# Sigmoid centres by tanh on GpSimd, the second attention's row norms on GpSimd and its row statistics a step later, and capacity blocks normed one at a time

## What is computed

```python
x = layernorm(x + L0_attn(x)); x = layernorm(x + L0_ffn(x))
x = layernorm(x + L1_attn(x)); x = layernorm(x + L1_ffn(x))
# L1_attn, what matters here (16 heads of width 8):
c = tanh(mixed_q @ wfq + bfq + (glo @ wfg + bfg))
P = sigmoid(sum(c * up)) * key_len      # centre of each row's window
Z = sigmoid(sum(c * uz)) * key_len      # its width
scores = q @ k.T / sqrt(8) - (j - P)**2 * 2 / Z**2
ctx = softmax(scores) @ v; return ctx @ wo + bo
# L1_ffn: each row goes to its best expert of 8, 160 slots an expert;
# rows that find no slot keep a zero contribution
```

## Time and profile before

| | before |
|---|---|
| median of 3 runs | 1567.42 us (1565.87 to 1569.64) |
| the profiled execution's own time | 1567.29 us |
| its span | 1565.5 us |
| PE busy | 1419.6 us, 91% |
| DVE busy | 1107.7 us, 71% |
| ACT busy | 996.5 us, 64% |
| POOL busy | 876.5 us, 56% |
| mean granted clock of PE | 0.959 of full |

### The profile page before, as it was taken

One profiled execution on the slowest core, in us unless ns is written; L12 is line 12 of the kernel. 1 busy time (PEld: TensorE's weight loads), 2 busy tenths in 40 slices (PEclk: granted clock), 3 DMA queues, 4 the chain that ended last, 5 costly groups with the idle time before them and its releaser, 6 DMA issues. The chain is left out here.

```text
span 1565.5 us, 37854 instructions
## 1 busy us (share of the span) xinstructions
PE 1419.6 (91%) x12163; PEld 805.0 (51%) x12163; DVE 1107.7 (71%) x2545; ACT 996.5 (64%) x2144; POOL 876.5 (56%) x1078
## 2 busy tenths in 40 slices
PE   5999999999999999999978999888889889897825
PEld 3666666666666666666646776623333333332215
DVE  5657676676766667676677898878887887888623
ACT  2666665666566566656647888747777777775612
POOL 4676777677677767767775445622342342342643
PEclk8999999999999999999989999969999999999967
DMA  6100000010000011000100000131111111112100
GB/s 194 32 22 22 24 26 20 20 27 20 20 21 26 20 20 27 20 20 20 27 14 5 0 0 1 41 87 49 45 34 52 36 35 50 30 43 73 29 14 27
DMA packets 74396, 50.83 MB, mean 32 GB/s; under 512 B 31099, under 2 KB 63728, under 8 KB 74192
## 3 DMA queue, kind: packets, MB, share of 16 engines
q1 hardware_dynamic: 71232, 45.70, 10.7%
q10 hardware_dynamic: 1760, 3.02, 0.6%
q0 software_dynamic: 1344, 1.33, 0.3%
HBM read 38.18 MB, written 13.28 MB: 33 GB/s over the span
## 5 line engine op out<-in xcount | busy, mean ns | idle before, releaser
L2031 DVE TENSOR_REDUCE a_nm<-a_s 128x1 f16<-128x512 f32 x512 | 323.7, 685 | 61.7 <-PE a_s L1853 59.0
L620 ACT ACTIVATE prob<-score_ps,nmax 128x512 f32<-128x512 f32 (+3 forms) x512 | 266.8, 528 | 149.5 <-DVE nmax L692 149.5
L692 DVE TENSOR_REDUCE nmax<-score_ps 128x1 f32<-128x512 f32 (+3 forms) x512 | 224.9, 480 | 184.5 <-PE score_ps L498 179.6
L1989 ACT ACTIVATE a_pt<-a_st 128x1024 f32<-128x1024 f32 x256 | 261.5, 1023 | 107.9 <-PE a_st L1857 106.4
L1853 PE MATMUL a_s<-a_kop,a_qop 64*128 64x512 f16 x512 | 185.9, 408 | 48.4 <-DVE a_nm L2031 40.9
L510 PE MATMUL pt_ps<-ident,prob 128*128 128x128 f32 x1280 | 182.7, 273 | 2.6 <-ACT pt L629 1.4
L629 ACT ACTIVATE pt<-pt_ps 128x512 f32<-128x512 f32 (+1 forms) x192 | 102.9, 536 | 123.7 <-PE pt_ps L510 123.7
L1889 PE MATMUL a_pv<-a_pt,a_vaug 128*32 128x256 f32 x2048 | 170.6, 406 | 8.9 <-ACT a_pvs L1994 7.6
L817 POOL TENSOR_SCALAR_AFFINE_SELECT k_h<-k 64x512 f16<-64x512 f32 x130 | 80.8, 622 | 170.7 <-ACT k L653 158.2
L1857 PE MATMUL a_st<-a_qop,a_kop 64*128 64x512 f16 x512 | 175.3, 399 | 0.0
L510 PEld LDWEIGHTS pt_ps<-ident,prob 128*128 128x128 f32 x1280 | 145.6, 141 | 35.2 <-ACT pt L629 1.6
(11 more groups left out here) (390 smaller groups left out, 3252.8 us busy)
## 6 DMA issues: line engine op xcount, KB each, us to landing
r_bc<-r_parts SPq DMA_DIRECT2D x128, 128.0 KB, 2.8
a_qop<-q_parts SPq DMA_DIRECT2D x64, 64.0 KB, 1.9
a_kop<-k_parts SPq DMA_DIRECT2D x64, 64.0 KB, 1.9
e_w<-in_L_ffn_w_dram SPq DMA_DIRECT2D x16, 256.0 KB, 3.3
x_tok<-in_L_attn_input_dram SPq DMA_DIRECT2D x4, 512.0 KB, 13.1
r_parts<-rsum SPq DMA_DIRECT2D x128, 2.0 KB, 2.1
q_parts<-a_q_h SPq DMA_DIRECT2D x16, 128.0 KB, 2.3
k_parts<-a_k_h SPq DMA_DIRECT2D x16, 128.0 KB, 2.3
```

Source lines behind the costliest of these rows:

```text
L620: ins = nc.scalar.activation(prob[h][:, P_OFF[c]:P_OFF[c] + w], score_ps[u][:, col:col + w], ACT.Exp, bias=nmax[h][:, c:c + 1], accum_out= ...
L692: ins = nc.vector.tensor_reduce(nmax[h][:, c:c + 1], score_ps[u][:, col:col + P * (c + 1)], AX.X, ALU.max, negate=True)
L1989: nc.scalar.activation(pt[kc % 2][r][:, :, :], st_ps[r][:, :, :], ACT.Exp, scale=1.0 / SC).then_inc(exp_done[r], 1)
L2031: nc.vector.tensor_reduce(nm[g % 2][:, c, hh:hh + 1], s_ps[j][:, :], AX.X, ALU.max, negate=True).then_inc(max_done[j], 1)
```

## The change

The centre is computed from a tanh: sigmoid(x) is 1/2 + tanh(x/2)/2. ACT now runs a Tanh on the centre's half and an Exp on the width's half of the same product. DVE's three operations for them are gone; POOL does a gate, the +1 on the width's half and one multiply-add that makes `a_cent`, ahead of its coefficients. DVE takes the row statistics of `OUT` in slot 11 in place of slot 10. The norm `a_xn` is made by POOL, behind `a_rstd` and ahead of the `a_scale` operations. In the capacity stage each block has its own `c_var`, `c_rstd`, `c_res` and scatter; POOL raises the next block's variance before it scatters the one before.

```diff
         def sigmoids(kind, b, nb):
             act.wait_ge(coef_done, nb)
             used(kind, b, "PZ")
-            nc.scalar.activation(epz[:, :, :].rearrange("p c h -> p (c h)"), misc[:, 0:QC * 2 * H1], ACT.Exp,
-                                 scale=-1.0).then_inc(misc_out, 1)
+            pz = misc[:, 0:QC * 2 * H1].rearrange("p (c h) -> p c h", c=QC)
+            nc.scalar.activation(epz[:, :, 0:H1], pz[:, :, 0:H1], ACT.Tanh, scale=0.5)
+            nc.scalar.activation(epz[:, :, H1:], pz[:, :, H1:], ACT.Exp, scale=-1.0).then_inc(misc_out, 1)
...
-        def centres(kind, b, nb):
-
-            steps = Steps(dve, cf_steps, 2 * nb)
-            dve.wait_ge(coef_done, nb)
-            dve.wait_ge(misc_out, use(kind, b, "PZ") + 1)
-            steps.step(nc.vector.tensor_scalar(epz[:, :, :], epz[:, :, :], 1.0, None, ALU.add))
-            steps.step(nc.vector.reciprocal(cent[:, :, :], epz[:, :, 0:H1]))
-            nc.vector.tensor_scalar(cent[:, :, :], cent[:, :, :], S / 32.0, -(S - 1) / 64, ALU.mult, ALU.add).then_inc(cent_done, 1)
...
             if j == 0:
-                pool.wait_ge(cent_done, nb + 1)
+                pool.wait_ge(misc_out, use(kind, b, "PZ") + 1)
+                pool_gate(nc, m, slice(0, P))
+                centre = Steps(pool, cf_steps, 2 * nb)
+                centre.done(nc.gpsimd.tensor_scalar(z, z, 1.0, None, ALU.add))
+                centre.step(nc.gpsimd.tensor_scalar(c, epz[:, :, 0:H1], S / 64.0, 1.0 / 64, ALU.mult, ALU.add))
...
+
+            def statistics(kind, b):
                 dve.wait_ge(misc_out, use(kind, b, "OUT") + 1)
-                layer_norm_stats(nc, dve, m, 2 * B + cb, y, st, mv)
-
-            def norm(cb):
-                layer_norm_apply(nc, dve, m, 2 * B + cb, y, mv, rstd, xn).then_inc(ln_dve, 1)
+                layer_norm_stats(nc, dve, m, 2 * B + b - 1, y, st, mv)
...
             def slot(kind, b, at):
                 if kind == "first" and at == 9:
                     last_stats()
+                if kind != "first" and at == 11:
+                    statistics(kind, b)
...
             def output(kind, b, cb):
                 layer_norm_gpsimd(nc, pool, m, 2 * B + cb, mv, ve, rstd)
                 pool.wait_ge(m.rstd_ready, 2 * B + cb + 1)
+                pool_gate(nc, m, slice(0, P))
+                for c in range(QC):
+                    last = nc.gpsimd.tensor_scalar(xn[:, c, :], y[:, c, :], mv[:, c, 0:1], rstd[:, c:c + 1], ALU.subtract, ALU.mult)
+                last.then_inc(ln_dve, 1)
...
                 steps.step(nc.vector.bn_aggr(mv[:, c, :], st[:, c, :]))
-
-            def variance(i):
-                two = slice(*PAIRS1[i])
-                nc.vector.tensor_tensor(var[:, two], mv[:, two, 1], m.eps[:, 0:PAIRS1[i][1] - PAIRS1[i][0]], ALU.add).then_inc(var_ready, 1)
...
+                nc.vector.tensor_tensor(var[:, c:c + 1], mv[:, c, 1:2], m.eps[:, 0:1], ALU.add).then_inc(var_ready, 1)
...
             for q in range(4):
                 tokens(q)
-            for i, blocks in enumerate(PAIRS1):
-                for c in range(*blocks):
-                    finish(c)
-                variance(i)
-                if i < len(PAIRS1) - 2:
-                    normalise(i)
-            for i in range(len(PAIRS1) - 2, len(PAIRS1)):
-                normalise(i)
+            finish(0)
+            for c in range(1, CH):
+                finish(c)
+                normalise(c - 1)
+            normalise(CH - 1)
...
             pool.wait_ge(tokens_done, 4)
-            for i in range(len(PAIRS1) - 2):
-                inverse_deviation(i)
-                scatter(i)
-            for i in range(len(PAIRS1) - 2, len(PAIRS1)):
-                inverse_deviation(i)
-            for i in range(len(PAIRS1) - 2, len(PAIRS1)):
-                scatter(i)
+            inverse_deviation(0)
+            for c in range(1, CH):
+                inverse_deviation(c)
+                scatter(c - 1)
+            scatter(CH - 1)
```

More of the change, by code:

```diff
@@ L1265, in ahead @@
                 if i in PARTS_AT:
[L1266 removed]
+                    turns["PZ_part"](PARTS_AT[i], "prep0", 0, 0)
                 if i == 0:
@@ L1375, in gauss_memory @@
                          "pool_steps"))
-    g.cf_steps, g.coef_done, g.vaug_done, g.ln_dve, g.pv_mm, g.parts_out, g.cent_done, g.cf_pool = (
-        sem(n) for n in ("cf_steps", "coef_done", "vaug_done", "ln_dve", "pv_mm", "parts_out", "cent_done", "cf_pool"))
+    g.cf_steps, g.coef_done, g.vaug_done, g.ln_dve, g.pv_mm, g.parts_out, g.cf_pool = (
+        sem(n) for n in ("cf_steps", "coef_done", "vaug_done", "ln_dve", "pv_mm", "parts_out", "cf_pool"))
     g.st_mm = [sem(f"st_mm{k}") for k in range(2)]
@@ L1559, in tokens @@
                 nc.vector.tensor_tensor(xt_l[:, :], misc[:, :], xt_h[:, :], ALU.subtract).then_inc(misc_out, 1)
[L1561 to L1570 removed]
+        return used, {"XT": tokens}
     def pool_steps_(pool):
@@ L2126, in slot @@
                     choose(CHOSEN_AT[kind, at])
-            schedule(dve, {"slot": slot, "RL": logits, "RC": place("RC"), "RD": place("RD"), **turns, "scores": maxima, "ctx": context, "OUT": output, "norm": norm})
+            schedule(dve, {"slot": slot, "RL": logits, "RC": place("RC"), "RD": place("RD"), **turns, "scores": maxima, "ctx": context, "OUT": output})
         @block.gpsimd
@@ L2333, in finish, with normalise @@
                 steps.step(nc.vector.bn_aggr(mv[:, c, :], st[:, c, :]))
-            def variance(i):
-                two = slice(*PAIRS1[i])
-                nc.vector.tensor_tensor(var[:, two], mv[:, two, 1], m.eps[:, 0:PAIRS1[i][1] - PAIRS1[i][0]], ALU.add).then_inc(var_ready, 1)
-            def normalise(i):
-                dve.wait_ge(rstd_ready, i + 1)
-                for c in range(*PAIRS1[i]):
-                    last = nc.vector.tensor_scalar(res[:, c, :], y[:, c, :], mv[:, c, 0:1], rstd[:, c:c + 1],
-                                                   ALU.subtract, ALU.mult)
-                last.then_inc(out_ready, 1)
+                nc.vector.tensor_tensor(var[:, c:c + 1], mv[:, c, 1:2], m.eps[:, 0:1], ALU.add).then_inc(var_ready, 1)
+            def normalise(c):
+                dve.wait_ge(rstd_ready, c + 1)
+                nc.vector.tensor_scalar(res[:, c, :], y[:, c, :], mv[:, c, 0:1], rstd[:, c:c + 1],
+                                        ALU.subtract, ALU.mult).then_inc(out_ready, 1)
             for q in range(4):
                 tokens(q)
-            for i, blocks in enumerate(PAIRS1):
-                for c in range(*blocks):
-                    finish(c)
-                variance(i)
-                if i < len(PAIRS1) - 2:
-                    normalise(i)
-            for i in range(len(PAIRS1) - 2, len(PAIRS1)):
-                normalise(i)
+            finish(0)
[3 more added lines that the diff above has]
+            normalise(CH - 1)
         @block.gpsimd
@@ L2359, in _, with inverse_deviation, scatter @@
             out_flat = out.rearrange("b s d -> (b s) d")
-            def inverse_deviation(i):
-                two = slice(*PAIRS1[i])
-                pool.wait_ge(var_ready, i + 1)
-                nc.gpsimd.tensor_tensor(rstd[:, two], var[:, two], m.mhalf[:, 0:PAIRS1[i][1] - PAIRS1[i][0]], ALU.pow).then_inc(rstd_ready, 1)
-            def scatter(i):
-                pool.wait_ge(out_ready, i + 1)
-                for c in range(*PAIRS1[i]):
-                    nc.gpsimd.indirect_dma_start(out=out_flat, out_offset=bass.IndirectOffsetOnAxis(ap=to_token[:, c:c + 1], axis=0),
-                                                 in_=res[:, c, :], in_offset=None, bounds_check=NT - 1,
-                                                 oob_is_err=False).then_inc(out_rows, 16)
-            pool.wait_ge(tokens_done, 4)
-            for i in range(len(PAIRS1) - 2):
-                inverse_deviation(i)
-                scatter(i)
-            for i in range(len(PAIRS1) - 2, len(PAIRS1)):
-                inverse_deviation(i)
-            for i in range(len(PAIRS1) - 2, len(PAIRS1)):
-                scatter(i)
+            def inverse_deviation(c):
+                pool.wait_ge(var_ready, c + 1)
+                nc.gpsimd.tensor_tensor(rstd[:, c:c + 1], var[:, c:c + 1], m.mhalf[:, 0:1], ALU.pow).then_inc(rstd_ready, 1)
+            def scatter(c):
+                pool.wait_ge(out_ready, c + 1)
+                nc.gpsimd.indirect_dma_start(out=out_flat, out_offset=bass.IndirectOffsetOnAxis(ap=to_token[:, c:c + 1], axis=0),
+                                             in_=res[:, c, :], in_offset=None, bounds_check=NT - 1,
+                                             oob_is_err=False).then_inc(out_rows, 16)
+            pool.wait_ge(tokens_done, 4)
+            inverse_deviation(0)
[3 more added lines that the diff above has]
+            scatter(CH - 1)
             pool.wait_ge(out_rows, 16 * CH)
```

9 lines of the change are left out of this document (4 added, 5 removed).

## The result

The changed kernel took **1577.12 us** (median of 6 runs, 1573.43 to 1578.29), the kernel before 1567.48 beside it: a ratio of 1.0059, 95% interval 1.0045 to 1.0072. It is 0.6% slower; I had forecast 0.5% faster. The profiled execution took 1576.94 with a span of 1575.1, 9.6 more than before's 1565.5.

What follows compares the result with a forecast made beforehand. PE was taken to bound the second attention, stopped by bursts on DVE. Middle batches -7.8, first -1.4, last +1.3, tail +1.3 and capacity stage -0.4 gave -7.0 from 1567.3: 1560.3 us, chance 0.46, range 1556 to 1567.

Steps and rivals of the forecast that it cites:

- the price p of a norm on POOL: Second attention: time from one new norm on POOL to the next, taken as 0.30 us, between 0.2 and 0.46.
- Rival 4: Slower: POOL's norm becomes the wait, in slot 14 through SP, in last batch and tail directly; 1573.6 us, chance 0.09.
- 32p - 19.3: Rival 4's sum for the whole change in us, by the norm's price p; even at 0.60, slower by 3.1 from 0.70.
- a collision at SBUF: Rival 4's possible cause: POOL and DVE slow each other at SBUF; at p = 0.8 the result is 1573.6 us.
- Middle batches: Six batches of the second attention: PE's 1.54 us stop becomes about 0.4 and 1.0; 1.3 us gained each, -7.8 us.
- rival 1: PE's lower clock goes altogether; middle batches reach their ceiling of 1.76 us, the first gains 2.2: 1556.7 us, chance 0.15.
- The ceiling: Middle batches: SP's maxima behind POOL's chain limit the gain to 1.76 us a batch, less 4(p - 0.30).
- First batch: First batch of the second attention: PE's 1.45 us wait for the centres goes, -1.4 us.
- Last batch and tail: Gate and four norms on POOL, E = 0.14 + 4p = 1.34 us, add 1.3 us in each, in the last batch at the router.
- Before the second attention: Centres on POOL cost 0, since PE waits there for DVE or the coefficients by no more than half a microsecond.
- Capacity stage: Single blocks of 2.28 us each start the ninth scatter at 1560.19 in place of 1560.59: -0.4 us.
- a shrinking gap: Capacity stage: if the gap ahead of a scatter shrinks from 0.68 to 0.30, 3.0 us more are gained.

Runs made afterwards that it cites:

- maxima_first: Changed kernel with SP's write of POOL's product held back to slot 13, behind the issue of the maxima of group 2: 0.9933 of the kernel before, 1567.8 us.
- norm_only: Kernel before with only the four row norms moved from DVE to POOL: 1.0020 of the kernel before, 3.2 us slower.
- first, third and fourth group: Follow-up runs on three of four chips, each timed beside the kernel before, which took 1578.8, 1577.9 and 1580.3 us there.
- second group: Follow-up runs on another chip (changed kernel again, its other parts, constants in the norm), each beside the kernel before, which took 1566.8 us there.
- blocks_only: Kernel before with only the single capacity blocks of the change: 0.9979 of the kernel before, 3.3 us faster.
- centres_only: Kernel before with only the centres moved to POOL by way of tanh, statistics and norm as before: 0.9976 of the kernel before, 1563.3 us.
- norm_back_maxima_first: Changed kernel with norm and first centres on DVE and SP's write moved to slot 13, behind the maxima of group 2: 0.9897 of the kernel before.
- norm_back: Changed kernel with the four row norms back on DVE at the end of slot 11: 0.9905 of the kernel before, 1563.5 us.

## Why the prediction was wrong

**The step that failed** is the price p of a norm on POOL, "nearest to the copy", 0.30. It measured 0.785, far above the upper end of 0.46. A copy moves four times the columns in 0.61 and a two-input operation of the norm's shape takes 0.46; the norm is dearer than either, and even two two-input operations over all four tiles (2.1 us) beat four norms (3.1). I had let "one tile and two columns" stand for the work, and no row of the trace had that form on POOL. The rule of the Trainium skill, GPSIMD Engine Reference, section 4.1 (two times slower for two-input work, roughly line-rate for one-input), has the right sign for this move. Neither of its sizes fits here: four norms take DVE 1.11 and POOL 3.14, 2.8 times as long.

**Rival 4 is what happened**: POOL's norm became the wait, through SP in slot 14 of the middle batches and through POOL in the tail, as it said; in the last batch too it was SP, and not POOL itself as it had said. By its sum, 32p - 19.3, p = 0.785 gives 1573.1, against 1576.9 of the profiled execution. That nearness is in part luck: the first row of the table and PE's clock in the second are 3.0 us that the sum doesn't have, and the capacity stage is 4.3 better than in it. The cause that it gave, a collision at SBUF, is not it: the norms are as long with DVE idle.

*Middle batches.* Where nothing waits in slot 14, with the norm on POOL as forecast (`maxima_first`), the five periods fall from 285.6 to 277.0 us, 1.7 each where I had 1.3: PE's clock stays up in four of them, as rival 1 said. The ceiling was right in its mechanism and too mild. At p = 0.785 it allows no gain but a loss of 0.2 us a batch; the loss is 0.7. The rest is PE's clock after the new stop: its scores take 0.60 in place of 0.39 and eight value products 1.08 in place of 0.64. In the three profiles of the changed kernel a period is 57.14 at full clock (the one there is), 57.8 to 58.0 at a mean of 0.97 and 58.6 to 58.7 at 0.94, with stops of 1.9 in all of them, so each low stretch costs 0.7 to 0.9. With constants in the norm POOL was only 0.17 us faster from `a_rstd` to `a_scale`, yet three of the five periods ran at full clock, and four are 1.0 us shorter. My sum had no term for a low clock behind a new stop.

*First batch.* -1.7 to a mark that itself lies 0.4 later (`a_rstd` starts 3.7 us behind the last product of `OUT` in place of 3.3): 2.1 gained, where I had 1.4.

*Last batch and tail.* I put E = 0.14 + 4p on both. In the tail, where POOL runs without a pause, E at 3.3 is what came: +3.0, and +3.1 in `norm_only`. In the last batch I had sought the cost at the router; with E above 3 the maxima of group 2 came first, and PE stopped for 5.46 us in place of 0.18 and 1.60.

*Before the second attention* I wrote 0, since PE waited there for less than half a microsecond. I looked at who waits for whom, not at what the moved work is put ahead of on its new engine: POOL's gate and centres (1.4 us) stand before a split of `hid_l`, and ACT's wait for the coefficients grew from 0.71 to 1.98. It cost 1.2 us to the first scores. The other 1.7 of the table's 2.9 came with a lower clock, which only some of the executions have.

*Capacity stage*: -0.4 by my sum, -4.7 measured, 1.2 of which is no part of the change (under the table). I carried the gap of 0.68 ahead of a scatter to every block. That gap was DVE's norm of a block behind a power that had only just ended; in the new order POOL scatters block c - 1 between the power of block c and its scatter, DVE norms block c beside that, and the gap is 0.18. So the stretch from the first scatter to the ninth, for which I had 0.6 more than before, is 2.1 less: 15.5 us in place of 17.65, with 1.83 a block behind the first two. The first scatter itself comes 1.3 earlier behind DVE's first `c_y`, where I had 1.0. I had named a shrinking gap, to 0.30, and 3.0 us for it, but had it only as a reserve.

## What to carry over

Before an elementwise step moves to GpSimd, look for a row of exactly its form, operand kinds and size there; without one, take as the upper end not the dearest neighbour in shape but a value from which the verdict turns, and give that end a real chance. Then ask what stands behind the moved work in every in-order queue, the transfer queue of SP above all: here one write issued two slots later was worth about 1% of the time with the slow norm (1.0048 against 0.9933), and nothing without it. A stop that goes also uncovers the next one, so a cost that is hidden when a part is tried alone need not be hidden in the whole.

## What the runs showed of the hardware

- On POOL a subtract-and-multiply of 128x128 with two row values takes 0.795 us, with constants 0.647, both as long with DVE idle as with DVE busy, to within 0.02 us, while a multiply-and-add of 128x64 with constants takes 0.245 (L1609) and a two-input operation of 128x512 1.04, a quarter of which is 0.26. Length here does not follow columns, and inputs count for less than the kind of operation. Why is open.
- On the chips of the first, third and fourth group ACT stops in the last batch or the tail for 1.9 to 3.6 us, two to four times, in every kernel profiled there; the profile names only "remote" as what ended the stop, and why is open. In the first profiles and in the second group there is none. The kernel before is 10 to 14 us slower on those three chips than in the first result and the second group, while the middle batches are as long (57.1 us on average in `blocks_only`). One of the stops:

```profile
1456.16 0.59 ACT L2000 ACTIVATE a_nm_t<-a_misc 4x512 f16<-4x512 f16 x1 [1.98 <-remote]
```

- The same code takes different times with PE's granted clock. The stretch from the first product of the mixture (L1110) to the gates' product takes 163.9 us at a mean clock of 0.99 (the kernel before, `centres_only`, `norm_back_maxima_first`) and 166.4 to 166.9 at 0.97 to 0.98 (all others). The stretch after it takes, with POOL's first centres, 31.9 at 1.00 or 33.6 at 0.95; without them it is 30.7 at 0.98 to 0.99. Which clock an execution gets there is not explained.
- PE's clock can fall after a stop of 1.5 to 1.9 us: for some 3 us scores then take 0.60 in place of 0.39. It does so in most batches with such a stop and not in all; in `norm_back`, with no stop above 0.81 in the five periods, it did so once.
